# Edge network of a graph kernel: the output norm's weight moves from GpSimd into the mixing matrix

## The reference

```
K_v = x @ Kv2v[h];  V_v = x @ Vv2v[h];  K_E = edge @ Ke2v[h];  V_E = edge @ Ve2v[h]
alpha = concat(K_v[dst] * K_v[src], K_v[dst] * K_E) / sqrt(128)
gate  = sigmoid(ln(alpha) * ln_g[h] + ln_b[h])
m = (concat(V_v[src], V_E) @ Wu[h] + bu[h]) * gate
m = leaky(ln(m @ Wm[h] + bm[h]) * mln_g[h] + mln_b[h])
head_h = segment_sum(m, dst)
```

## Time and profile before

| | us |
|---|---|
| median of 3 runs | 13353.01 |
| lowest, highest | 13352.68, 13353.71 |
| span of the profiled execution | 13346.2 |

### The profile page before, as it was taken

How to read it: one execution, slowest core, us unless ns; L and a number is a source line. 1 busy time by engine, 2 the same in 40 slices (tenths; PEclk the granted TensorE clock), 3 DMA queues, 4 the chain that set the end, 5 groups by cost and what they waited for, 6 DMA issues and landing times.

```text
span 13346.2 us, 181640 instructions
## 1 busy us (share of the span) xinstructions
PE 9273.5 (69%) x45190; PEld 6132.3 (46%) x45190; DVE 9007.8 (67%) x20368; ACT 5821.3 (44%) x11467; POOL 9313.9 (70%) x6569
## 2 busy tenths in 40 slices
PE   1344444444475888888888888888888887779886
PEld 0233333333224665666666666665666565333222
DVE  3233333333207888888888888888888887157996
ACT  0111111111003666666666666666666665026332
POOL 1688888888504888888888888888888885000553
PEclk9999999999997999999999999989999998989997
DMA  9766666666783333333343333333334333869553
GB/s 412 233 159 149 152 152 151 153 149 152 198 360 123 120 119 120 119 119 120 119 119 119 120 119 119 120 119 120 119 119 120 119 119 97 347 260 330 177 186 104
DMA packets 1232552, 2147.34 MB, mean 161 GB/s; under 512 B 345985, under 2 KB 768210, under 8 KB 1218579
## 3 DMA queue, kind: packets, MB, share of 16 engines
q1 hardware_dynamic: 838120, 1657.69, 36.0%
q0 software_dynamic: 390240, 484.27, 16.5%
q10 hardware_dynamic: 4048, 3.51, 0.1%
HBM read 1652.11 MB, written 492.84 MB: 161 GB/s over the span
## 4 chain that ended last, share of the span: by engine, by line
POOL 41%; issue 23%; PE 11%; DVE 8%; DMA 8%; ACT 4%; SPq 3%; DVEq 1%; POOLq 1%; another core or an unknown queue 0%; ACTq 0%; PEldq 0%
POOL arena L1367 21%; POOL adj L1406 13%; POOL arena L1419 5%; DMA arena<-adj 4%; SPq L1471 3%; PE psum L1278 2%; DMA adj<-put_val,put_idx 2%; ACT arena L984 2%; POOL arena L1422 2%; PE psum L1201 1%; PE psum L1136 1%; DVE arena L901 1%; PE psum L1290 1%; PE psum L1214 1%; PE psum L1191 1%
## 5 line engine op out<-in xcount | busy, mean ns | idle before, releaser
L1406 POOL DMA_INDIRECT adj<-put_val,put_idx x1616 | 2639.9, 1634 | 832.4 <-issue 461.0
L984 ACT ACTIVATE arena<-arena 128x128 f32<-128x128 f32 x6464 | 2657.2, 488 | 296.2 <-DVE arena L775 111.5
L1115 PE MATMUL psum<-ke,arena 64*128 64x256 f32 x3232 | 1451.5, 640 | 1871.3 <-DMA arena<-in_edge_t 1871.3
L1367 POOL DMA_INDIRECT arena<-table1q,idx_dst x1616 | 2255.6, 1396 | 492.4 <-issue 492.4
L1367 POOL DMA_INDIRECT arena<-table,idx_blk x1616 | 1898.1, 1175 | 432.2 <-issue 376.2
L1115 PEld LDWEIGHTS psum<-ke,arena 64*128 64x128 f32 x3232 | 1041.2, 330 | 2281.2 <-issue 2013.9
L1201 PEld LDWEIGHTS psum<-wm,arena 128*128 128x128 f32 x12928 | 1751.3, 203 | 608.0 <-issue 509.3
L990 ACT ACTIVATE arena<-psum,cols 128x512 f32<-128x512 f32 x1616 | 1248.4, 773 | 1717.6 <-PE psum L1183 1382.5
L1191 PE MATMUL psum<-arena,wvu 128*128 128x512 f32 x3232 | 1890.9, 670 | 84.6 <-DVE arena L704 59.1
L1214 PE MATMUL psum<-arena 128*128 128x128 f32 x6464 | 1116.7, 325 | 1118.3 <-DVE arena L731 1104.4
L1201 PE MATMUL psum<-wm,arena 128*128 128x64 f32 x12928 | 1793.8, 285 | 5.9 <-issue 4.6
(11 more groups left out here) (210 smaller groups left out, 12378.0 us busy)
## 6 DMA issues: line engine op xcount, KB each, us to landing
arena<-adj SPq DMA_DIRECT2D x192, 1568.0 KB, 12.5
arena<-adj SPq DMA_DIRECT2D x336, 896.0 KB, 4.7
kept_keys<-arena SPq DMA_DIRECT2D x404, 512.0 KB
arena<-kept_keys SPq DMA_DIRECT2D x404, 512.0 KB
adj<-arena SPq DMA_DIRECT2D x98, 1568.0 KB
arena<-in_edge_t SPq DMA_DIRECT2D x808, 128.0 KB
kept_hot<-arena SPq DMA_DIRECT2D x404, 256.0 KB
arena<-kept_hot SPq DMA_DIRECT2D x404, 256.0 KB
```

The costliest lines, as they stand in the source:

```text
L984: A.activation(to, at_, ACT.Identity, bias=shift[z][:, n:n + 1], scale=rstd[z][:, n:n + 1]).then_inc(normed, 1)
L1115: last = M.matmul(psum[:, 2 + 2 * z + j, t * H * D:(t + 1) * H * D], edge0[z][:, 2 * j + t, :], ke[D:P, :], start=True, stop=True)
L1367: K.indirect_dma_start(out=dst[:, t, :], out_offset=None, in_=table, in_offset=bass.IndirectOffsetOnAxis(ap=idx[:, t:t + 1], axis=0)).then ...
L1406: K.indirect_dma_start(out=adj, out_offset=bass.IndirectOffsetOnAxis(ap=put_idx[s][:, j:j + 1], axis=0), in_=put_val[s][:, j:j + 1], in_of ...
```

## The change

The mixing weights become two sets side by side in a new tile `wmg`: column set 1 is `wm` less its mean (as before), column set 0 the same times `mg`. The bias gets the same two sets. The mixed tile is therefore 512 columns instead of 256 and fills a PSUM bank alone. ScalarE squares the plain columns and copies the weighted ones, tile by tile. The variance is thus that of the plain output, and `y` has its weight already when VectorE scales it. GpSimd's multiplication is gone; only `mb` is added. The preparation moves ahead of the first counting of the destinations, and three small tiles that it uses once are placed in the unused end of `acc`.

```
# VectorE, once, right after the inputs have landed
+            link(V.tensor_tensor(wmg[:, :, 0, :], wmg[:, :, 1, :], mg[:, :].rearrange("p (h d) -> p h d", h=H), ALU.mult))
...
# VectorE, the body of sweep1
-                    after(dve, o_done, 2 * (i - 2))
+                    after(dve, o_done, G * (i - 2))
-                    dve.wait_ge(y_affine, 2 * (i - 3))
+                    dve.wait_ge(y_affine, i - 3)
-                    dve.wait_ge(o_taken, 2 * (i - 2))
+                    dve.wait_ge(o_taken, G * (i - 2))
...
# ScalarE
-                def take_o(j):
-                    act.wait_ge(o_done, 2 * (i - 2) + j + 1)
-                    pair = slice(2 * j * H, 2 * (j + 1) * H)
-                    ps = psum[:, 6, :].rearrange("p (q d) -> p q d", d=D)
-                    A.activation(o_sq[z][:, pair, 0:D], ps, ACT.Square, scale=(P / D) ** 0.5)
-                    A.activation(o_sb[z][:, pair, :], ps, ACT.Copy).then_inc(o_taken, 1)
+                def take_o(t):
+                    act.wait_ge(o_done, G * (i - 2) + t + 1)
+                    own = slice(t * H, (t + 1) * H)
+                    ps = psum[:, 6, :].rearrange("p (q a d) -> p q a d", a=2, d=D)
+                    A.activation(o_sq[z][:, own, 0:D], ps[:, :, 1, :], ACT.Square, scale=(P / D) ** 0.5)
+                    A.activation(o_sb[z][:, own, :], ps[:, :, 0, :], ACT.Copy).then_inc(o_taken, 1)
...
# TensorE
-                def o_pair(j):
-                    pe.wait_ge(gm_ready, H * (i - 1))
-                    after(pe, o_taken, 2 * (i - 2) + j)
-                    for t in range(2):
-                        at_ = t * H * D
-
-                        for h in range(H):
-                            M.matmul(psum[:, 6, at_ + h * D:at_ + (h + 1) * D], gm[z][:, h, 2 * j + t, :],
-                                     wm[:, h, :], start=h == 0, stop=False)
-                        last = M.matmul(psum[:, 6, at_:at_ + H * D], ones3[:, :], bm_parts[:, :],
-                                        start=False, stop=True)
+                def o_tile(t):
+                    after(pe, o_taken, G * (i - 2) + t)
+                    M.matmul(psum[:, 6, :], ones3[:, :], bm_parts[:, :], start=True, stop=False)
+                    pe.wait_ge(gm_ready, H * (i - 1))
+                    for h in range(H):
+                        last = M.matmul(psum[:, 6, h * 2 * D:(h + 1) * 2 * D], gm[z][:, h, t, :],
+                                        wmg[:, h, :, :].rearrange("p a d -> p (a d)"), start=False, stop=h == H - 1)
...
# GpSimd
-                K.tensor_tensor(y4, y4, mg[:, :].unsqueeze(1).to_broadcast([P, G, H * D]),
-                                ALU.mult).then_inc(y_affine, 1)
-                pool.wait_ge(y_affine, 2 * g + 1)
```

More of the change, by code:

```diff
@@ L141, in gnn @@
         vecs = sb("vecs", [D, 6])
[L142 to L146, removed]
+        wmg = sb("wmg", [P, H, 2, D])
+        bm_part = [sb(f"bm_part{i}", [1, 2 * H * D], BF16) for i in range(3)]
+        bm_parts = sb("bm_parts", [3, 2 * H * D], BF16)
         ones3 = sb("ones3", [3, P], BF16)
@@ L506, in _ @@
             dve.wait_ge(s_load, ALL_IN)
+            link(V.tensor_reduce(small[:, 0:H], wm[:, :, :], AX, ALU.add))
+            link(V.tensor_scalar(small[:, 0:H], small[:, 0:H], 1.0 / D, None, ALU.mult))
+            link(V.tensor_tensor(wmg[:, :, 1, :], wm[:, :, :],
+                                 small[:, 0:H].unsqueeze(2).to_broadcast([P, H, D]), ALU.subtract))
+            link(V.tensor_tensor(wmg[:, :, 0, :], wmg[:, :, 1, :], mg[:, :].rearrange("p (h d) -> p h d", h=H), ALU.mult))
+            link(V.tensor_reduce(small[0:1, 0:H], bm_row, AX, ALU.add))
+            link(V.tensor_scalar(small[0:1, 0:H], small[0:1, 0:H], 1.0 / D, None, ALU.mult))
+            link(V.tensor_tensor(bm_rest[:, :, 1, :], bm_row,
+                                 small[0:1, 0:H].unsqueeze(2).to_broadcast([1, H, D]), ALU.subtract))
+            link(V.tensor_tensor(bm_rest[:, :, 0, :], bm_rest[:, :, 1, :],
+                                 mg[0:1, :].rearrange("p (h d) -> p h d", h=H), ALU.mult))
+            for i in range(3):
+                part = bm_part[i][:, :].rearrange("p (h a d) -> p h a d", h=H, a=2)
+                link(V.tensor_copy(part, bm_rest), mark="bm_parts")
+                if i < 2:
+                    link(V.tensor_copy(bm_up, part))
+                    link(V.tensor_tensor(bm_rest, bm_rest, bm_up, ALU.subtract))
             link(V.tensor_copy(base_f, base_b.rearrange("p (k two) -> p k two", two=T // RUNS)[:, :, 0]))
@@ L560, in _ @@
             link(V.tensor_copy(wvu[:, :, :], psum[:, 1, :].rearrange("p (h n) -> p h n", h=H)), mark="fused")
[L561 to L574, removed]
             evict("table0", lambda c, ps: V.tensor_tensor(
@@ L1010, in sweep1 @@
                     sigmoid(1)
-                    norm(i - 1, (s + 3) % U, odd, 3)
-                    sigmoid(2)
                 if now[2]:
@@ L1016, in sweep1 @@
                 if now[1]:
+                    norm(i - 1, (s + 3) % U, odd, 3)
+                    sigmoid(2)
+                if now[2]:
+                    take_o(1)
+                if now[1]:
                     sigmoid(3)
+                if now[2]:
+                    take_o(2)
                 if now[0]:
@@ L1021, in sweep1 @@
                 if now[2]:
-                    take_o(1)
+                    take_o(3)
             steps(act, sweep1, NG, 4, 2)
@@ L1227, in sweep1 @@
                 if now[2]:
-                    o_pair(0)
+                    o_tile(0)
                 if now[1]:
@@ L1231, in sweep1 @@
                     m_u(2)
+                if now[2]:
+                    o_tile(1)
                 if now[4]:
@@ L1237, in sweep1 @@
                 if now[2]:
-                    o_pair(1)
+                    o_tile(2)
                 if now[4]:
                     sums(1)
+                if now[2]:
+                    o_tile(3)
             steps(pe, sweep1, NG, 8, 4)
```

7 lines of the change are left out of this document (6 added, 1 removed).

## The result

The changed kernel takes 13937.08 us (median of 4 runs, 13876.25 to 13975.6) against 13353.36 (13352.68 to 13368.43) for the one before: a ratio of 1.0429, 95% interval 1.0412 to 1.0446. It is 584 us slower where 430 us less was forecast. (The 6.8 us given for the kernel before compares the span of one execution with the median of others, and is mostly the spread between them.)

What follows compares the result with a forecast made beforehand. GpSimd was taken as the bound at 17.50 us a group, VectorE next at 16.42 to 16.46. Span 13346.2 less 437 or 420, plus 6.8, gave 12916 to 12933, taken as 12923; likeliest case's range 12895 to 12985, overall 12885 to 13070.

Steps and rivals of the forecast that it cites:

- The 6.8 us: Difference between the profiled execution's span and the median of the runs, added on top of the forecast span.
- GpSimd's multiplication goes: GpSimd in the edge network saves 2.45 us a group, needs 15.05 instead of 17.50, and then waits for `y`.
- VectorE bounds at 16.42 to 16.46: VectorE's loop work becomes the next bound at that many us a group, gaining 437 or 420 us.
- TensorE's width: Mixing matmuls of 128 instead of 64 columns cost nothing; the doubled bias matmul costs 0.4 us a group.
- ScalarE's takes: Eight 256-column instructions of 0.41 us replace four of 512 columns: +0.9 us a group, covered by idle time.
- The preparation: Extra small steps ahead of the counting of destinations cost nothing; 2 to 8 us without the cover there.
- The port: GpSimd's addition over VectorE's large steps could hold VectorE up to 1.15 us; placing kept it clear; chance 0.05.
- rival C: No gain: GpSimd's addition holds VectorE through the shared port by up to 1.15 us, 13350 us; chance 0.05.
- the new waits: Each mixed tile waits for the take before it, closing a TensorE, ScalarE, VectorE loop of 15.2 us, under VectorE's 16.08.
- start earlier by as much: GpSimd's index copy and eight gathers, queued behind its addition, start 4.4 us earlier.
- The loop: Sums, last mixings, takes, norms, gate and message in a circle: TensorE 4.3, ScalarE 8.7, VectorE 2.2, sum 15.2 us.
- Rival B: Slower: dearer takes (+0.8), low clock (+1.4) and handovers (+1.0) bring the loop to 18.4 us, 13720 us; chance 0.06.

Runs made afterwards that it cites:

- experiment 5: Changed kernel, with GpSimd waiting for VectorE's message step before the four destination gathers: 12849.04 us, ratio 0.9638.
- experiments 5 to 7: Changed kernel with GpSimd waiting for the message (12849.04 us) or landed table gathers (12985.02), its addition split (12880.5), or narrower destination rows or key load (12874.54 to 12876.67).
- e10_before_no_mult_wait: Kernel before, without GpSimd's multiplication and with GpSimd waiting for the message before the destination gathers: 12851.42 us, ratio 0.9638.
- 7: Changed kernel with destination rows of 64 or 512 bytes instead of 1024 (12876.67, 12875.55 us), or 16 of each 256 key columns loaded (12874.54).
- 10: Key load delayed until its group's table gathers landed: in the changed kernel 14092.07 us, in the changed kernel with the message wait 12928.74.
- experiments 4 to 9: Changed kernel with five gathers, GpSimd waits, split addition, narrower rows or keys, or start-only wait; kernel before with the message wait, with or without multiplication: 12832.97 to 13936.54 us.
- `e5` to `e12`: Changed kernel with message or landing wait, split addition, narrower rows or keys; kernel before with message wait, without or with multiplication: 12849.04 to 13336.57 us.
- experiment 3: Changed kernel with a scratch addition of 512 columns on GpSimd between the fourth and fifth gather: 13151.22 us, ratio 0.9858.
- experiment 2: Kernel before with GpSimd's multiplication left out, the weight not applied: 14018.04 us, ratio 1.0500.

## Why the prediction was wrong

The steps on the engines held:

- *GpSimd's multiplication goes:* right, and GpSimd then waits for `y` (L1430 behind L791, 334.9 us).
- *VectorE bounds at 16.42 to 16.46:* right in kind, shown by experiment 5: period 16.31, 94% busy. 0.11 to 0.15 us a group was too much, 45 to 60 us in all; where they went was not followed up. This alone would have put the time below the stated range: 12849 us, and by its ratio 0.9638 x 13353.36 = 12870, under 12885.
- *TensorE's width:* right. Eight matmuls of the mixing hold the queue for 7037.89 - 7036.89 = 1.00 us by the starts in the trace, as the earlier trace rows gave for the sums, and the bias matmul for 7036.89 - 7036.57 = 0.32 instead of 0.21, 0.4 us a group, the middle taken.
- *ScalarE's takes:* forecast 0.41 us each, measured 0.383 and 0.379 (L1003, L1004): +0.7 us a group, not +0.9.
- *The preparation:* right, no cost is seen. In experiment 5, with the same preparation, the first L737 starts at 4207.0, before the first L731 of the kernel before (4220.3).
- *The port:* right for the change (rival C did not happen).
- *The 6.8 us on top:* 1.8 us lie around the instructions in every run; 5 us, too small to matter.

The step that failed is **the new waits**, with the sentence ahead of it that the gathers "start earlier by as much". The loop was summed with handovers of 0.2 us, every count arriving when its work is done. The runs show takes 0 and 1 late by 1.85 and 1.78 us. These two takes stand in no term of the loop, which enters ScalarE at take 2. But ScalarE works in order: norm 3 and sigmoid 2 stand behind take 0, sigmoid 3, take 2 and norm 0 behind take 1, so every late count is added to ScalarE's own round, 11.9 us of work and 7.0 us of waits for TensorE of which 4.1 are late counts, and the period is 19.04. (15.2 + 1.85 + 1.78 = 18.8 comes near it; the loop as summed doesn't contain the two, so that is no proof.) Rival B had the right sign and place, by three small costs (18.4 us, 13720) of which at most the clock came true (0.89 in these 1000 us): takes were cheaper, and where no count was late the handovers took 0.03 to 0.07 us. Its right sign was luck.

What could have been read beforehand: in the kernel before, TensorE's counts were already late now and then, the second take by 0.14 us in the mean. GpSimd's train was looser there, eight gathers in 7042.82 - 7030.40 = 12.4 us, since VectorE's large steps stretched two of them (1.82 and 2.73 us), against 7034.57 - 7024.30 = 10.3 after. The placing of the gathers was worked out for the ports and for when the data is needed; that their transfers would fall beside SP's key load was not asked. In the kernel before no key load runs beside a gather at all.

**What is shown and what stays open.** Shown: the loss comes from TensorE's counts, 2 to 4 us late in the example and up to 6.5 in the loop; the kernels of experiments 5 to 7 and `e10_before_no_mult_wait` are without them, and take 12849 to 12985. The key load at full width and the wide destination rows are both needed (7), and moving the load onto these gathers makes the counts late where they weren't (10).

Not shown: how either holds up TensorE's counts. Three things on record limit the guess. A queue that grows behind GpSimd, which my expectations for experiments 4 to 9 took for the cause, is against the packets in the traces: the last bytes of a gather have landed 1.5 to 1.9 us after the end of its issue, on average for each of the eight, in the changed kernel as in the one before. Busy DMA engines are not enough, nor is a key load beside gathered rows of any kind (experiment 5: 0.92 of DMA share, 1.23 us a group beside table rows, no late count). Of the 333 takes that were over 1 us late after the change, 179 (tile 0) had no byte of the key load beside them, only gathered rows; that these too vanish with narrow keys I can't explain.

One rival is tested by no run: the recording. Every run here has a span and a clock from the profile, so none was made without it. And the records suffer where the counts do: in the eight kernels without one count over 1 us late (`e5` to `e12`) 98.6% or more of VectorE's counts were recorded, in all others, the kernel before among them, 59 to 80%. Either one thing holds up both the counts and the records, or writing the records is itself what holds up TensorE. The runs can't tell which, and so don't show that a run without recording loses the 584 us.

## What to carry to other kernels

When an engine that issues DMAs gets faster, lay its transfers, and not only its instructions, beside those of every other queue, and ask which handover between engines stands under the overlap. A wait in the profile that no instruction explains ("remote" on one core), on the chain that ended last, can be the sign of it. Counts missing from the trace are another, and they showed it here before it cost anything. The cure may be a wait on the engine that has time: one line on GpSimd turned 13937 us into 12849 (ratios 1.0429 and 0.9638).

## What the runs showed of the hardware that was not expected

- Semaphore counts of TensorE came 2 to 4 us after the modelled end of the work (7031.60 to 7035.84, four of them within 0.2 us of each other), those of VectorE and ScalarE within 0.01 us, with DMA at 0.87 to 0.93. In experiment 5, with DMA at 0.88 and 0.92, they came in time.
- The loss doesn't go by the bytes: destination rows of 64 and of 512 bytes give the same time (12876.67 and 12875.55), 1024 bytes 13937.
- VectorE's counts on record fall from 98.6% or more to 59 to 80% in the very kernels that have late counts.
- An instruction of GpSimd stretched one of VectorE from 1.22 to 2.23 us (experiment 3).
- The granted clock was 0.916 in the mean after the change, 0.868 in experiment 2 and 0.976 in experiment 5, and 0.930 in the kernel before.
- A copy out of PSUM takes 0.383 us for 256 columns, 0.594 for 512.
